# Gated graph network on one core: nine instead of eight of layer one's sixteen superblocks from dense products

## The reference

```python
h = jnp.maximum(_layernorm(x, axis=-1), 0.0)
h = h @ lin_w.T + lin_b
for i in range(3):
    m = h @ weight[i]
    agg = jax.ops.segment_sum(m[src], dst, num_segments=n_nodes)
    h = gru_cell(agg, h, w_ih, w_hh, b_ih, b_hh)
return x + h
```

## Time and profile before

| | |
|---|---|
| median of 3 runs | 3921.93 us (3919.45 to 3923.62) |
| the profiled execution | 3925.55 us, span 3921.8 us |
| busy: PE / ACT / DVE / POOL | 3421.9 / 2976.9 / 2840.9 / 2804.9 us |
| granted PE clock, mean | 0.95 |
| moved by DMA | 757.84 MB, mean 193 GB/s |

### The profile page before, as it was taken

One profiled execution on the slowest core, in us unless ns is written; L12 is line 12 of the kernel. 1 busy time (PEld: TensorE's weight loads), 2 busy tenths in 40 slices (PEclk: granted clock), 3 DMA queues, 4 the chain that ended last, 5 costly groups with the idle time before them and its releaser, 6 DMA issues.

```text
span 3921.8 us, 74234 instructions
## 1 busy us (share of the span) xinstructions
PE 3421.9 (87%) x24980; PEld 2703.0 (69%) x24981; DVE 2840.9 (72%) x8112; ACT 2976.9 (76%) x4189; POOL 2804.9 (72%) x2814
## 2 busy tenths in 40 slices
PE   6288898888887999996999989999969999999996
PEld 4166666666665777775777777777757777777775
DVE  7477787877776777775777777777757777777774
ACT  4177888878887878786788878788857878878783
POOL 4777777777777777742777777677727777777776
PEclk8699999999998999998999999999989999999998
DMA  8345565655557766665676667666766666666664
GB/s 273 107 154 183 186 197 196 201 183 185 184 187 247 218 192 205 193 185 170 190 214 197 209 190 209 187 200 196 216 178 185 201 195 204 202 192 202 194 199 121
DMA packets 462173, 757.84 MB, mean 193 GB/s; under 512 B 67432, under 2 KB 339432, under 8 KB 461800
## 3 DMA queue, kind: packets, MB, share of 16 engines
q1 hardware_dynamic: 214456, 405.22, 32.2%
q0 software_dynamic: 132096, 270.71, 24.8%
q10 hardware_dynamic: 115248, 77.10, 6.3%
HBM read 577.29 MB, written 175.47 MB: 192 GB/s over the span
## 4 chain that ended last, share of the span: by engine, by line
POOL 45%; PE 19%; issue 17%; ACT 7%; DVE 6%; DMA 3%; DVEq 2%; ACTq 0%; POOLq 0%; SPq 0%
POOL ring_region L565 45%; PE psum L860 13%; ACT wide_counts L682 6%; DMA states<-temps 2%; DVE aggT L1188 2%; PE psum L815 1%; DVEq L1140 1%; PE psum L827 1%; DVE message_halves L1285 1%; DVE message_halves L1283 1%; PE psum L785 1%; PE psum L786 1%; PE psum L758 1%; PE psum L787 1%; DVE temps L1217 1%
## 5 line engine op out<-in xcount | busy, mean ns | idle before, releaser
L565 POOL DMA_INDIRECT ring_region<-messages,edge_src x2752 | 2750.9, 1000 | 1027.0 <-issue 833.6
L860 PE MATMUL psum<-wide_counts,message_halves 128*128 128x504 f32 x7840 | 1935.7, 404 | 115.3 <-DVE message_halves L1285 109.7
L682 ACT CAST wide_counts<-messages_region 128x1008 fp32r<-128x1008 uint8 x1680 | 1835.4, 1170 | 259.6 <-PE psum L860 205.2
L860 PEld LDWEIGHTS psum<-wide_counts,message_halves 128*128 128x128 f32 x7840 | 1478.4, 192 | 471.6 <-ACT wide_counts L682 103.5
L1285 DVE TENSOR_TENSOR message_halves<-messages_region,message_halves 128x256 fp32r<-128x256 f32 x1680 | 790.7, 471 | 57.9
L842 PE MATMUL psum<-quad_onehots,block_onehots 128*128 128x238 bf16 (+2 forms) x6272 | 773.9, 274 | 62.9 <-ACT quad_counts L709 35.7
L709 ACT CAST quad_counts<-psum 128x504 uint8<-128x504 f32 x1568 | 773.6, 638 | 65.1 <-PE psum L842 62.7
L842 PEld LDWEIGHTS psum<-quad_onehots,block_onehots 128*128 128x128 bf16 x6272 | 546.1, 101 | 276.0 <-issue 45.2
L1283 DVE CAST message_halves<-messages_region 128x256 fp32r<-128x256 f32 x1680 | 639.6, 381 | 55.4 <-PE psum L860 33.8
L1249 DVE TENSOR_SCALAR quad_onehots<-iota_quad,count_keys 128x1666 bf16<-128x1666 f16 (+2 forms) x896 | 528.3, 652 | 0.0
L827 PE MATMUL psum<-onehot,ring_region 128*128 128x36 bf16 x8256 | 264.1, 179 | 216.9 <-DMA ring_region<-messages,edge_src 209.4
(11 more groups left out here) (104 smaller groups left out, 1534.0 us busy)
## 6 DMA issues: line engine op xcount, KB each, us to landing
messages_region<-counts SPq DMA_DIRECT2D x560, 441.0 KB
counts<-quad_counts SPq DMA_DIRECT2D x224, 441.0 KB
ring_region<-messages,edge_src POOLq DMA_INDIRECT x2752
messages<-pieces_out ACTq DMA_DIRECT2D x98, 192.0 KB
messages_region<-plain SPq DMA_DIRECT2D x21, 896.0 KB, 8.1
temps<-states ACTq DMA_DIRECT2D x98, 128.0 KB
states<-temps ACTq DMA_DIRECT2D x98, 128.0 KB
plain<-temps ACTq DMA_DIRECT2D x98, 128.0 KB
```

The source lines that it names most:

```text
L565: nc.gpsimd.indirect_dma_start(out=rows[:, n % RING, h * QC + c, :], out_offset=None, in_=messages[layer], in_offset=bass.IndirectOffsetOn ...
L682: nc.scalar.copy(wide_counts[:, v % UBUF, :, cols], stage[v % ABUF][:, :, cols]).then_inc(s_wide, 1)
L860: mm = nc.tensor.matmul(psum[:, 6 + kg % 2, 0:DQ * W], halves[:, v % UBUF, b % HB, half * P:(half + 1) * P], wide_counts[:, v % UBUF, :, c ...
```

## The change

One constant is changed. `FIRST_DENSE` goes from 8/16 to 9/16, so `KD` goes from 8 to 9, `KG` from 8 to 7 and `TURN` from 104 to 91.

```diff
 LEAD = 4
 TAIL_SPARE = 4
-FIRST_DENSE = 1 / 2
+FIRST_DENSE = 9 / 16
 BUILD_FROM = 6
 BUILD_SPARE = 2
```

## The result

The changed kernel takes 3900.09 us (median of 5 runs, 3896.86 to 3902.2), and the kernel before 3920.07 us (median of 5, 3915.78 to 3923.62). The ratio is 0.9943, with a 95% interval of 0.9932 to 0.9954, so it is faster by 22 us (18 to 27 us). The forecast was 18 us less. The two profiled executions lie a little further apart, 3925.55 and 3896.86 us, with spans of 3921.8 and 3895.0 us.

A forecast was written before the change was run, and what follows sets the result against it. POOL bounds counting and PE the dense steps; with the change PE sets both. Counting -79, transition -2, a wait -2.4 and one more superblock +66 sum to -17 us, from 3921.93 to 3904 us; range 3878 to 3928 us (8 in 10).

The forecast's parts named there:

- What sets the stretch: Counting stretch: POOL sets it before; after the change PE, at 931 us against POOL's 879 us, sets it.
- the waits for ACT and DVE: Counting stretch: PE's waits before count matmuls, 62.9 us before, put at 60 us instead of 55 us by count of tiles.
- Waits for rows after step 6: Counting stretch: PE's waits for gathered rows, 51.8 us before, were to shrink to a remaining 4 us.
- low-clock excess: Counting stretch: extra time of steps at 1.2 GHz behind waits for rows; 12 us to go, bounds 0 and 16 us.
- eight such waits: Counting stretch: PE's waits for rows of 2.3 to 4.3 us, with steps behind them 1.0 to 2.1 us too long.
- From counting to dense: Last count to first dense matmul, 22.8 us before: with rows at hand PE could begin after 20.8 us, 2 us less.
- the single wait of 2.4 us: PE's wait for rows at 1283.98 us, after dense work begins, was to go because the ring is full.
- One more dense superblock: Layer one's dense steps: one more PE cycle, costing 66 us, with POOL's 62 us as lower bound and 68 us above.
- Layers two and three: After layer one: they were to keep their steps, and a change in their length would make the prediction wrong.
- The late one-hot matrices: Rival, counting stretch: DVE makes one-hot matrices too late for PE, up to 41 us, giving 3941 us; chance 0.13.
- The slower gathers: Rival, counting stretch: denser one-hot making slows POOL's gathers past 1.42 us each, giving 3935 us; 1.33 expected; chance 0.03.
- One figure of the range: Forecast's own case: PE sets counting at 925 to 950 us, giving 3884 to 3914 us, chance 0.60.

## Why the prediction was right

**What sets the stretch** held. POOL set the counting with eight dense superblocks and does not with nine (66 us against 3 us for the same gathers left out), and PE sets the dense steps in both.

**The sum.** The counting stretch was to take 940 us and took 931.4 us, so 8.6 us of the profiled gain were not foreseen. By its terms: the waits for ACT and DVE came to 60.6 us, where the text had 60 us. Waits for rows after step 6 came to zero, where it had 4 us. The steps' low-clock excess fell by about 16 us, from 35 to 19 us, where it had 12 us. In the clock record the stretch had fifteen pieces at 1.2 GHz, 54.4 us together, and has seven, 23.8 us together. The prediction counted the eight behind waits for rows, and these are gone, as it said. It overlooked the other seven, which stood behind waits of 1.9 to 2.5 us for ACT or DVE (the first in the burst at 219.59 us). The changed kernel again has seven, six behind waits for ACT and one behind a wait for DVE. One is at 1124.40 us, where 64 matmuls take 9.06 us. Nor does every wait bring it. The prediction's "eight such waits" for rows of 2.3 to 4.3 us are nine, and the ninth, 3.10 us at 331.25 us, had a granted clock of 1.00 behind it. The Trainium skill (TensorE: Matmul & The Clock Gate, "HAM oscillation — how this bites in real kernels") describes the low clock behind waits for data between bursts of matmuls. The traces agree for eight of these nine waits, and they show it behind waits for other engines as well.

**From counting to dense** was to give 2 us and gave 3.4 us, and the single wait of 2.4 us behind it came out as 3.0 us over the first superblock.

**One more dense superblock** was to cost 66 us, and the seven cost 462.5 - 395.9 = 66.6 us more than six.

**Layers two and three** kept their length within 0.3 us.

**The checks that the text named.** The last count was to stand near 1142 us and stands at 1133.29 us. POOL's waits for sums while counting were to be 15 to 35 us and are 18.2 us.

**The timed difference** of 22 us is 4 to 5 us smaller than the 26.8 us of the two spans. One execution of each was profiled, and runs of one kernel differ by up to 8 us here. The sum of 17 us is 9 to 10 us short of the two executions whose terms it adds up, and 5 us short of the timed gain (the forecast itself, 18 us, is 4 us short). That it came so near to the timed gain is partly luck. That the time fell by about this much, and why, is not.

**The rivals.** The late one-hot matrices did not decide, for PE's waits for DVE are 17.8 us where they were 26.8 us. The run with less DVE work shows that they are nevertheless not free. The slower gathers came as bounded: 1029 ns instead of 1019 ns. One figure of the range doesn't follow from its own terms: a stretch of 925 us gives 3889 us, not 3884 us. Nothing hangs on it.

## What to carry to other kernels

When an engine heads the chain, first find how far behind the second one is: subtract the second engine's waits for the first from the stretch. Here that was 52 us out of 1019 us, plus about 16 us of low clock that went with the waits. Some 20 us of PE's own work and waits left with the 13 steps. Together they capped what the steps could give in their stretch at 88 us, instead of the 138 us that POOL needed for them. Once the bound has moved, look for the new engine's idle time elsewhere. Filling PE's idle start, worth 9 us while POOL was the bound, was worth 40 us afterwards.

## What the runs showed of the hardware

Busy time of PE in this profile is not all its own. With less work on ACT per round the same 6268 matmuls were busy for 53 us less (715.0 against 768.1 us), and 76 of them at full clock for 8.44 us instead of 9.17 us. So matmuls that follow a slow reader of PSUM look busy and not idle.

The granted clock fell from 2.4 to 1.2 GHz behind six waits of 2.0 to 3.0 us for ACT, as it did behind waits for gathered rows, and the steps became about 1.3 us longer (1.0 to 2.1 us behind the waits for rows). It did not behind five other waits for ACT of 2.4 to 3.0 us in the same kernel. Two bursts of 64 matmuls in the changed kernel, at 1124.40 us behind a wait of 2.43 us (shown above) and at 979.90 us behind one of 2.92 us, by timeline and then by stretch (the granted clock follows POOL's count):

```profile
979.90 7.80 PE L842 MATMUL psum<-quad_onehots,block_onehots 128*128 128x266 bf16 x64 [2.92 <-ACT quad_counts L709]
...
1124.40:1133.30 8.90, 8.90 (x65) 6.59 (x66) 3.81 (x10) 8.13 (x17) 5.32 (x6) 0.81 0.38 113
...
979.90:987.70 7.80, 7.79 (x71) 5.51 (x72) 6.53 (x18) 7.80 (x17) 5.41 (x6) 1.00 0.37 109
```

So the length of the wait alone does not decide. What else does, these runs do not show.
